# Attention scores of a head pair: two stacked full-height products after transfers, or three half-height products side by side without them

## The reference

```python
qkv = x @ w_qkv                                   # 128 -> 3 * 16 heads * 64
q, k, v = ...                                     # (b, 16, 512, 64)
sim = einsum('bhid,bhjd->bhij', q * 64 ** -0.5, k)
sim = sim - abs(i - j) * slope[h]                 # per head
sim = where(causal, -max, sim)
attn = softmax(sim, axis=-1)
out = einsum('bhij,bhjd->bhid', attn, v)          # then out @ w_out + b_out
```

## Time and profile before

| | |
|---|---|
| median of three runs | 1647.11 us |
| the profiled execution | 1647.01 us |
| its span, first to last instruction | 1645.2 us |
| PE busy | 1580.9 us, 96% |
| ACT busy | 1295.4 us, 79% |
| DVE busy | 1180.6 us, 72% |
| POOL busy | 948.1 us, 58% |
| share of 16 DMA engines used by SP's queue | 45.1% |

### The profile page before, as it was taken

One profiled execution on the slowest core, in us unless ns is written; L12 is line 12 of the kernel. 1 busy time (PEld: TensorE's weight loads), 2 busy tenths in 40 slices (PEclk: granted clock), 3 DMA queues, 4 the chain that ended last, 5 costly groups with the idle time before them and its releaser, 6 DMA issues.

```text
span 1645.2 us, 34916 instructions
## 1 busy us (share of the span) xinstructions
PE 1580.9 (96%) x10932; PEld 1294.8 (79%) x10932; DVE 1180.6 (72%) x4264; ACT 1295.4 (79%) x3468; POOL 948.1 (58%) x1252
## 2 busy tenths in 40 slices
PE   6899999999999999999999999999999999999996
PEld 5777878788787887878788787887878788787875
DVE  6575886858778586785858769586785858768565
ACT  5787887878878787887878878788887878878782
POOL 2555665656656566565656656566565656656451
PEclk9899999999999999999999999999999999999999
DMA  2444554444545444544444545444544444544540
GB/s 85 99 105 103 106 113 97 103 91 99 118 88 122 89 92 100 116 104 96 99 105 94 123 88 113 90 100 100 116 101 94 100 107 96 113 90 103 107 87 14
DMA packets 80054, 163.17 MB, mean 99 GB/s; under 512 B 12800, under 2 KB 30848, under 8 KB 79744
## 3 DMA queue, kind: packets, MB, share of 16 engines
q1 hardware_dynamic: 79872, 160.94, 45.1%
HBM read 6.88 MB, written 4.19 MB: 7 GB/s over the span
## 4 chain that ended last, share of the span: by engine, by line
PE 78%; DVE 11%; DMA 4%; issue 4%; ACT 1%; SPq 1%; POOL 0%; POOLq 0%; DVEq 0%; ACTq 0%
PE bank L430 13%; PE bank L415 13%; PE bank L401 8%; PE bank L402 8%; PE bank L381 7%; PE bank L475 7%; PE bank L483 7%; PE bank L382 6%; PE bank L385 6%; DMA queries<-queries 4%; DVE drive L680 2%; DVE negsc L620 2%; DVE spikes L677 1%; DVE queries L741 1%; DVE negmem L683 1%
## 5 line engine op out<-in xcount | busy, mean ns | idle before, releaser
L1030 POOL TENSOR_TENSOR prob<-prob,rsum 128x512 f32<-128x512 f32 (+3 forms) x1024 | 761.9, 760 | 629.6 <-DVE rsum L629 628.6
L888 ACT ACTIVATE prob<-negsc,negmax 128x512 f32<-128x512 f32 (+3 forms) x1024 | 575.8, 565 | 107.6 <-DVE negmax L620 101.6
L620 DVE CUSTOM_DVE_ANT_0 negsc<-bank,alibi 128x512 f32<-128x512 f32 (+3 forms) x1024 | 466.4, 474 | 0.7 <-PE bank L402 0.3
L899 ACT COPY probT<-bank 128x512 f32<-128x512 f32 x640 | 362.9, 588 | 64.1 <-PE bank L415 63.9
L401 PE MATMUL bank<-keys,queries 128*128 128x256 f32 (+2 forms) x1024 | 347.1, 350 | 30.7 <-issue 26.6
L629 DVE RECIPROCAL rsum<-sums 128x1 f32<-128x1 f32 (+1 forms) x768 | 121.3, 158 | 353.0 <-PE bank L402 335.1
L415 PE MATMUL bank<-ident,prob 128*128 128x128 f32 x2560 | 364.3, 273 | 0.7 <-POOL prob L1030 0.7
L415 PEld LDWEIGHTS bank<-ident,prob 128*128 128x128 f32 x2560 | 301.0, 140 | 25.4 <-POOL prob L1030 4.0
L402 PE MATMUL bank<-keys,queries 128*128 128x256 f32 (+2 forms) x1024 | 318.6, 325 | 0.0
L430 PE MATMUL bank<-probT,vals 128*64 128x512 f32 (+3 forms) x2048 | 303.9, 439 | 2.3 <-ACT probT L899 2.3
L430 PEld LDWEIGHTS bank<-probT,vals 128*64 128x64 f32 x2048 | 135.5, 136 | 161.2 <-issue 135.6
(11 more groups left out here) (102 smaller groups left out, 2219.9 us busy)
## 6 DMA issues: line engine op xcount, KB each, us to landing
queries<-queries SPq DMA_DIRECT2D x381, 256.0 KB, 2.9
keys<-k_lo SPq DMA_DIRECT2D x254, 128.0 KB, 2.6
keys<-keys SPq DMA_DIRECT2D x127, 128.0 KB, 2.3
x_in<-in_L_attn_x_dram SPq DMA_DIRECT2D x16, 256.0 KB, 3.2
out_dram<-x SPq DMA_DIRECT2D x15, 256.0 KB, 2.4
prob<-in_L_attn_w_qkv_dram SPq DMA_DIRECT2D x1, 1536.0 KB, 9.2
wo<-in_L_attn_w_out_dram SPq DMA_DIRECT2D x1, 512.0 KB, 10.5
probT<-in_L_ffn_W_fc_dram SPq DMA_DIRECT2D x1, 256.0 KB, 3.3
```

Of the source, the lines that this page charges most:

```text
L620: ins = dve.tensor_tensor_reduce(negsc[:, k % 3, col:col + WIDTH[i]], src, alibi[:, 2 * p + h, N - WIDTH[i]:N], 1.0, MASKED, ALU.add, ALU.min,
L888: ins = act.activation(prob[:, p % 2, h, PCOL[i]:PCOL[i] + WIDTH[i]], negsc[:, k % 3, col:col + WIDTH[i]], ACT.Exp, bias=negmax[:, p % 2, ...
L899: act.copy(probT[:, turn_slot(p, t), :], turn_bank[(len(TRUNS) * p + t) % 2][:, :]).then_inc(s_turned_out, 1)
L1030: ins = pool.tensor_tensor(pr, pr, rsum[:, p % 2, seg:seg + 1].to_broadcast([P, WIDTH[i]]), ALU.mult)
```

## The change

Scores are made two tiles at a time, one of each head, in beats 0, 2 and 4. A product uses only the 64 partitions where its head lies, so nothing needs to be copied: three products (q_hi·k_hi, q_hi·k_lo, q_lo·k_hi) for head 0 and three for head 1, taking turns, into two score banks. A pair takes 24 matmuls. The transfers, the doubled weights and the doubled products of the start go away; q_lo and k_lo are written where they are used. The order of the tiles now takes both heads' like tiles in turn, and tile k+1 is made with tile k, after tile k-2 has been read.

```diff
-TILES = [[(1, 3)], [(1, 2)], [(0, 3)], [(0, 2)], [(1, 1), (0, 1)], [(1, 0), (0, 0)]]
+TILES = [[(0, 3)], [(1, 3)], [(0, 2)], [(1, 2)], [(0, 1), (0, 0)], [(1, 1), (1, 0)]]
...
-TRUNS = [[(1, 2), (0, 2)], [(1, 1), (1, 3)], [(0, 1), (0, 3)], [(1, 0)], [(0, 0)]]
+TRUNS = [[(0, 2), (1, 2)], [(0, 1), (0, 3)], [(1, 1), (1, 3)], [(0, 0)], [(1, 0)]]
...
-        queries = sb("queries", [P, 2, 2, 2, N], F32R)
-        q_hi, q_lo = queries[:, :, :, 0, :], queries[:, :, :, 1, :]
-        keys = sb("keys", [P, 2, 2, N], F32R)
-        k_lo = sb("k_lo", [P, N], F32R)
+        q_hi = sb("q_hi", [P, 2, N], F32R)
+        q_lo = sb("q_lo", [P, 2, N], F32R)
+        k_hi = sb("k_hi", [P, 2, N], F32R)
+        k_lo = sb("k_lo", [P, 2, N], F32R)
...
-            def place(b, p):
...
-                for s in range(PAIRS):
-                    if s < PAIRS - 1 or last >= 1:
-                        place(*((b, s + 1) if s < PAIRS - 1 else (b + 1, 0)))
...
-            def scores(b, p, k, par):
-                first, i = TILES[k][0]
-                if i == NT - 1 and (b, p) == (0, 0):
-                    pe.wait_ge(s_first[first], 2)
-                elif i == NT - 1:
-                    pe.wait_ge(s_twice[p % 2][first], twice_no(b, p, first))
-                    pe.wait_ge(s_keys[p % 2][first], keys_no(b, p, first))
-                wait(pe, s_biased, tile_no(b, p, k - 3))
-                rows = slice(i * P, (i + 1) * P)
-                width = max(WIDTH[i], 2 * P)
-                for n, (h, _) in enumerate(TILES[k]):
-                    dst = score_bank[k % 3][:, score_col(k, n):score_col(k, n) + width]
-                    pe.matmul(dst, q_hi[:, p % 2, h, rows], keys[:, p % 2, h, 0:width], start=True, stop=False)
-                    mm = pe.matmul(dst, q_lo[:, p % 2, h, rows], keys[:, p % 2, h, 0:width], start=False, stop=True)
-                mm.then_inc(s_scores, 1)
+            def scores(b, p, k):
+                i = TILES[k][0][1]
+                if i == NT - 1:
+                    pe.wait_ge(s_qlo, qk_no(b, p))
+                    pe.wait_ge(s_klo, qk_no(b, p))
+                wait(pe, s_biased, tile_no(b, p, k - 2))
+                both = [score_bank[(k + h) % 3] for h in range(2)]
+                for n, (_, i) in enumerate(TILES[k]):
+                    rows = slice(i * P, (i + 1) * P)
+                    width = max(WIDTH[i], 2 * P)
+                    for q, keys in ((q_hi, k_hi), (q_hi, k_lo), (q_lo, k_hi)):
+                        for h in range(2):
+                            dims = slice(h * DH, (h + 1) * DH)
+                            mm = pe.matmul(both[h][:, score_col(k, n):score_col(k, n) + width], q[dims, p % 2, rows],
+                                           keys[dims, p % 2, 0:width], start=(q is q_hi and keys is k_hi), stop=(q is q_lo))
+                            if q is q_lo and n == len(TILES[k]) - 1:
+                                mm.then_inc(s_scores, 1)
...
-                    if exists(b, s):
-                        scores(b, s, k, par)
+                    if k % 2 == 0 and exists(b, s):
+                        scores(b, s, k)
...
-                    bb, pp = before(b, p, 1)
-                    for h in range(2):
-                        wait(dve, s_keys[pp % 2][h], keys_no(bb, pp, h))
-                    dve.tensor_tensor(k_lo[:, :], src, keys[:, p % 2, 0, :].bitcast(F32), ALU.subtract).then_inc(s_klo, 1)
+                    dve.tensor_tensor(k_lo[:, p % 2, :], src, k_hi[:, p % 2, :].bitcast(F32), ALU.subtract).then_inc(s_klo, 1)
```

More of the change, by code:

```diff
@@ L71 @@
 ]
-FIRST = [(1, "q"), (1, "k"), (0, "q"), (0, "k")]
 SPIKE1 = [(2, 5), (2, 5), (3, 0), (3, 1), (3, 4), (3, 4), (4, 4), (4, 4), (4, 4), (4, 4), (5, 0), (5, 3), (5, 4), (5, 4)]
@@ L92, in macaron_kernel @@
         last_out_bank = side_bank + score_bank[0:2]
-        first_bank = turn_bank + side_bank
         def end_bank(kind, i):
@@ L150, in macaron_kernel @@
         attT = sb("attT", [P, PAIRS + 2, N])
-        twice_view = queries[:, 1, :, :, :].rearrange("p h l n -> p (h l n)")
-        def weights_twice(kind, low, h):
-            return (("qk".index(kind) * 2 + low) * 2 + h) * P
         w_raw = prob[:, :, :, :].rearrange("p a h n -> p (a h n)")[:, 0:3 * INNER]
@@ L163, in macaron_kernel @@
         s_wfc, s_wproj, s_wqkv, s_wo, s_stored = (sem(n) for n in ("s_wfc", "s_wproj", "s_wqkv", "s_wo", "s_stored"))
-        s_keys = [[sem(f"s_keys_{n}{h}") for h in range(2)] for n in ("even", "odd")]
-        s_twice = [[sem(f"s_twice_{n}{h}") for h in range(2)] for n in ("even", "odd")]
         s_xin = [sem("s_xin_even"), sem("s_xin_odd")]
@@ L183, in macaron_kernel @@
         s_block_half = sem("s_block_half")
-        s_wvlo, s_wtwice, s_dup, s_dup_hi, s_first = sem("s_wvlo"), sem("s_wtwice"), sem("s_dup"), sem("s_dup_hi"), [sem("s_first0"), sem("s_first1")]
+        s_wvlo = sem("s_wvlo")
         s_out, s_x1, s_x1b, s_x2, s_x3 = (sem(n) for n in ("s_out", "s_x1", "s_x1b", "s_x2", "s_x3"))
@@ L202, in qk_no @@
         def qk_no(b, p):
[L204 to L212, removed]
+            return b * PAIRS + p + 1
         def pv_no(b, p, n):
@@ L239, in freed @@
                 p = (s + 1) % PAIRS
-                return ((s_qlo if kind == "q" else s_klo), qk_no(b, p)) if qk_no(b, p) > 0 else (s_first[0], 2)
+                return (s_qlo if kind == "q" else s_klo), qk_no(b, p)
             if kind == "v":
@@ L277, in run @@
             tail()
-        def q_first(p):
-            return [kind for s, _, kind, _, _ in SIDE if s == (p - 1) % PAIRS and kind in "qk"] == ["q", "k"]
         def side_at(s, k, offsets):
@@ L542, in chain, with first_pair @@
                         side(n, kind, i, 0, b, s, b % 2, None, end_bank(kind, i))
+            def first_pair():
+                for n, (s, _, kind, _, off) in enumerate(SIDE):
+                    if off == 1 and kind in "qk":
+                        pe.wait_ge(s_wlo, 1 + "qk".index(kind))
+                        side(n, kind, 0, 0, 0, s, 0, None)
             def head():
@@ L564, in head @@
                 pe.wait_ge(s_xhi[2], 1)
[L565 to L570, removed]
+                first_pair()
                 pe.wait_ge(s_wvlo, 1)
@@ L740, in low_half @@
                     dve.wait_ge(s_qhi, qk_no(b, p))
-                    dve.tensor_tensor(q_lo[:, p % 2, 0, :], src, q_hi[:, p % 2, 0, :].bitcast(F32), ALU.subtract).then_inc(s_qlo, 1)
+                    dve.tensor_tensor(q_lo[:, p % 2, :], src, q_hi[:, p % 2, :].bitcast(F32), ALU.subtract).then_inc(s_qlo, 1)
                 elif kind == "k":
@@ L841, in head @@
                 low_half(number("t2"), "t2", 0, 0, 0, 0, end_bank("t2", 0))
[L842 to L849, removed]
+                for n, (s, _, kind, _, off) in enumerate(SIDE):
+                    if off == 1 and kind in "qk":
+                        low_half(n, kind, 0, 0, s, 0)
                 dve.wait_ge(s_alibi, 1)
@@ L913, in high_half @@
                     p = (s + 1) % PAIRS
-                    dst, made, done = (q_hi, s_q, s_qhi) if kind == "q" else (keys, s_k, s_khi)
+                    dst, made, done = (q_hi, s_q, s_qhi) if kind == "q" else (k_hi, s_k, s_khi)
                     act.wait_ge(made, qk_no(b, p))
-                    act.copy(dst[:, p % 2, 0, :], src).then_inc(done, 1)
+                    act.copy(dst[:, p % 2, :], src).then_inc(done, 1)
                 elif kind == "v":
@@ L976, in head @@
                 act.copy(wproj[:, :, :].rearrange("p t c -> p (t c)"), score_bank[1][:, :]).then_inc(s_wproj_out, 1)
[L977 to L981, removed]
                 chain(0, ("t1", "fc1", "y1"))
@@ L988, in head @@
                 act.wait_ge(s_const, 3)
-                act.wait_ge(s_whi, 3)
-                copy_twice("q", 0, wq_hi)
-                copy_twice("k", 0, wk_hi)
                 for h in range(HEADS):
@@ L994, in head @@
                 ins.then_inc(s_alibi, 1)
-                act.wait_ge(s_wlo, 1)
-                copy_twice("q", 1, wq_lo)
                 chain(0, ("t2",))
-                act.wait_ge(s_wlo, 2)
-                copy_twice("k", 1, wk_lo)
-                for m, (h, kind) in enumerate(FIRST):
-                    act.wait_ge(s_dup, m + 1)
-                    if kind == "q":
-                        ins = act.copy(q_hi[:, 0, h, :], first_bank[m][:, :])
-                    else:
-                        ins = act.copy(keys[:, 0, h, :], first_bank[m][:, :])
-                    ins.then_inc(s_dup_hi, 1)
+                for n, (s, _, kind, _, off) in enumerate(SIDE):
+                    if off == 1 and kind in "qk":
+                        high_half(n, kind, 0, 0, s, 0)
                 act.wait_ge(s_wlo, 2)
```

## The result

The changed kernel takes 1689.1 us (median of four, 1688.18 to 1689.52) against 1647.5 (1646.47 to 1648.98): a ratio of 1.0251, with a 95% interval of 1.0233 to 1.0269. It is 42 us slower; forecast were 1692 us, 45 slower.

What follows compares the result with a forecast made beforehand. PE, busy 96% of the span, was taken as the bound. On the 1645.2 us span, -82 + 154 - 31 + 5 - 1 = +45 gave 1690, with 1.8 us around it 1692 us, 2.7% slower; range 1605 to 1795.

Steps and rivals of the forecast that it cites:

- Stream, -82 us: PE's score products: two heads' half-height products run at the same time, 0.64 us less a pair, 82 us over 128 pairs.
- Change of shape, +154 us: PE's three half-height score groups a pair: each pays 0.40 us for going in and out, 154 us (0 to 192).
- Wait on transfers, -31 us: PE's waits before line 401, mostly one at each batch's first scores, disappear: 31 us less (0 to 31).
- Traffic, 0: Apart from PE's wait, the transfers' disappearance was to give nothing, as SP is free.
- New wait on DVE, +5 us: At beat 4 PE needs tile 2 read, before it needed tile 1: 5 us more (0 to 20).
- The start, -1 us: Kernel start: two products fewer of three matmuls, shorter train of casts and remainders, about 1 us less (0 to 2).
- One of the signs: Expected in the profile after: few waits of PE at beat 4 ended by DVE's line for the maximum.
- no price: Rival: PE takes half-height products between full-height ones like any other, the 154 us is gone, 1538 us; chance 0.10.
- half the price: Rival: a half-height group's change of shape costs about half, 0.20 us, giving 1615 us; chance 0.09.
- one after the other: Rival: the two heads' half-height products don't overlap on PE, 246 us more, 1938 us; chance 0.08.
- held by loads: Rival: heads run side by side, but PE's weight loads hold the passes, 91 us, 1783 us; chance 0.08.
- the wait that stays: Rival: scores at a batch's start wait for something else, so the 31 us stay, 1723 us; chance 0.05.

Runs made afterwards that it cites:

- a_full: The changed kernel with its 24 score products a pair on all 128 partitions instead of 64: 1781.7 us, ratio 1.0809 to the kernel before.
- a_heads: The changed kernel with head 0's three products, then head 1's three, instead of taking turns: 1690.5 us, ratio 1.0257 to the kernel before.
- b_half: The kernel before with one extra 256-column product on 64 partitions ahead of the scores in beats 1, 3 and 5: 1795.8 us, ratio 1.0899.
- b_full: The kernel before with one extra 256-column product on all 128 partitions ahead of the scores in beats 1, 3 and 5: 1674.8 us, ratio 1.0165.
- a_waits: The changed kernel with six dummy transfers a pair put back and PE waiting for the first four: 1723.0 us, ratio 1.0449 to the kernel before.
- a_transfers: The changed kernel with six dummy transfers a pair put back that nothing waits for: 1688.6 us, ratio 1.0244 to the kernel before.
- b_wait2: The kernel before, with PE in beats 0, 2 and 4 waiting until score tile k-2, not k-3, is read: 1665.4 us, ratio 1.0113.

## Why the prediction was right

The bound was read rightly: PE's list is the time, and its terms add up. The signs and mechanisms of the large terms held. Two sizes were off, the price of the shape (too large) and the new wait on DVE (too small), and they hid each other.

- *Stream, -82 us.* Held. The distances in the profile after are those of one head's product, and counted at the undisturbed 0.231, 0.174 and 0.118 us for 512, 384 and 256 columns the scores' stream falls by 82 us, from 328.2 to 246.1, and a_full shows what is lost without the overlap. That half-height would follow the half-width row was a choice, and a_full and a_heads bear it out.
- *Change of shape, +154 us.* That there is a price held: b_half against b_full isolates it. The size was too large. Added up over the 382 whole groups of the profile after, without their waits, the marks make 139 us, 0.36 a group. The price of the way out came from a block whose weight loads last 0.19 us (line 475), but most groups are followed by turns, whose loads last 0.14 us, and such a group costs 0.35 (0.34 above); and the full-height scores of before had not been quite free, some 10 us, so net about 129. I had taken 0.40 and nothing. What goes on inside PE at a change, the drain and the open load of my reading, no run takes apart.
- *Wait on transfers, -31 us.* The wait went as forecast, from 30.7 us to nothing. But the prediction let nothing take its place ("what is late next there is PE itself"), and two things did: PE comes into a batch some 1.9 us earlier and then meets DVE's list at beat 4 (next term but one), and already at beat 0 the turns wait for ACT's copy, 3.3 us in 15 times, a wait that the kernel before does not have:

```profile
635.85 0.63 PE L351 MATMUL bank<-ident,prob 128*128 128x128 f32 x4 [0.22 <-ACT probT L829]
```

  a_waits puts the wait back for 0.9 us in an undisturbed batch, not 1.75.
- *Traffic, 0.* Held: a_transfers.
- *New wait on DVE, +5 us.* This step was mis-sized. In the trace after, the starts of beat 4's groups exceed the bare change of shape by 23 us in all: some 12 in slot 0, 9 in slot 4, 2 in slot 7. The sum looked at slots 4 and 7. In slot 7 the credit that I gave was due: the gap of 0.46 us is all but gone. In slot 4 some 0.57 of the 0.76 stayed. Slot 0, which idles the most, was not in the sum at all: PE reaches it early because the transfers' wait is gone. b_wait2 gives 18.5 us for the tightened wait alone, near 23, but in other slots (above), so it shows the kind of wait and not its size here. The tiles' order changed too, and no run isolates that. In slot 4 DVE did not idle less for it: it took the remainders of the next queries and keys ahead of tile 2 (starts on DVE, then PE's group):

```profile
692.44 0.69 DVE L683 TENSOR_TENSOR k_lo<-bank,k_hi 128x512 fp32r<-128x512 f32 x1 [0.34 <-ACT k_hi L846]
693.05 0.68 DVE L679 TENSOR_TENSOR q_lo<-bank,q_hi 128x512 fp32r<-128x512 f32 x1
693.72 0.54 DVE L558 CUSTOM_DVE_ANT_0 negsc<-bank,alibi 128x384 f32<-128x384 f32 x1
694.18 0.08 DVE L558 DVE_READ_ACCUMULATOR2_ANT negmax<- 128x1 f32 x1
```

  DVE takes its list in order, so a tile that is ready earlier is not read earlier when other work stands before it. Slot 0, once a batch of 101.9 us:

```profile
640.04 0.39 PE L336 MATMUL bank<-k_hi,q_hi 64*128 64x256 f32 x2 [0.75 <-DVE negmax L558]
741.91 0.38 PE L336 MATMUL bank<-k_hi,q_hi 64*128 64x256 f32 x2 [0.74 <-DVE negmax L558]
```

- *The start, -1 us.* Held: six matmuls of 512 columns fewer, 1.4 us of stream.

With the measured sizes the sum is -82 - 1.4 + 129 - 31 + 23 + 3.3 = +41 us of the span's 42.4. So the closeness of the forecast, 3 us, is in part luck: the price of the shape was 25 us too high, and the waits for DVE and ACT 21 us too low. One of the signs that the prediction named did come out against it: PE has not a few waits at beat 4 for DVE's maximum but 34, 20.7 us. The rivals fell: no price and half the price by b_half, one after the other by a_full, held by loads by the distances after, the wait that stays by the missing row.

The Trainium skill's rule that a change of tiling mode drains the engine ("TensorEngine Tiling (Array Packing)", Key Properties) fits b_half: its half-height products cost some 0.35 us each beyond full-height ones. Its sentence that loads overlap matmuls in flight only in another row group ("TensorE: Matmul & The Clock Gate", The mechanism) is not borne out, taken by itself: inside a group each head has new weights for every product, whose load is recorded with 0.18 us, and the products still follow each other at 0.23, 0.18 and 0.12 us, as full-height ones do.

## What to carry to other kernels

Count changes of the array's shape as you count matmuls: here halving the height made the scores' stream a quarter shorter (2.56 to 1.92 us a pair, 0.64 less) and lost 1.08 us a pair at three groups of 0.36. By these figures a single group a pair would have gained, as an estimate, 0.28 us; no run tried it. The transfers cost by the wait for the last of them and not by their bytes. And a wait that is taken away or tightened moves PE against every other engine: go through all slots of the trace of before and ask what PE meets next when it comes earlier, and don't add such terms as if each stood alone.

## What had not been expected of the hardware

The text ahead says that each engine runs its list in order. PE did not keep to that between the two halves of the array: with three products of one half ahead of three of the other, the halves ran side by side at the same distances, 0.28 and 0.18 us, and the kernel took 1690.5 us, as with the products taking turns.
